# Context rows taken relative to the last one, and short matmul groups given new places in the tile

## What is computed

```python
x = x + xattn(layernorm(x), ctx)    # 16 heads of 16; softmax over 257 context rows
x = x + attn(layernorm(x))          # rms-norm, rotary q and k, sigmoid weights divided by their sum
x = x + moe(layernorm(x))           # gate 256 -> 8, top 1, capacity 160, experts 256 -> 1024 -> 256, gelu

def xattn(query, ctx):
    q, k, v = heads(query @ Wq.T + bq), heads(ctx @ Wk.T + bk), heads(ctx @ Wv.T + bv)
    return merge(softmax(q @ k.T) @ v) @ Wo.T + bo
```

## Time and profile before

| | before |
|---|---|
| median of 3 runs | 1319.5 us (1315.08 to 1319.97) |
| the profiled execution | 1326.8 us, of which its span is 1324.9 us |
| PE matmul / weight load busy | 1160.6 us (88%) / 980.9 us (74%) |
| DVE / ACT / POOL busy | 851.6 us (64%) / 801.9 us (61%) / 568.9 us (43%) |
| mean granted clock of TensorE | 0.946 of full speed |

### The profile page before, as it was taken

How to read it: one execution, slowest core, us unless ns; L and a number is a source line. 1 busy time by engine, 2 the same in 40 slices (tenths; PEclk the granted TensorE clock), 3 DMA queues, 4 the chain that set the end, 5 groups by cost and what they waited for, 6 DMA issues and landing times. The chain is left out here.

```text
span 1324.9 us, 43348 instructions
## 1 busy us (share of the span) xinstructions
PE 1160.6 (88%) x17169; PEld 980.9 (74%) x17169; DVE 851.6 (64%) x2395; ACT 801.9 (61%) x2347; POOL 568.9 (43%) x1045
## 2 busy tenths in 40 slices
PE   6898988989889889999988988998999988874897
PEld 5677777777777777777777777777787777752796
DVE  4667777776776677766677766777666667653111
ACT  5677666666666666666666766766656666632121
POOL 2344444454554444445445444444444544432021
PEclk9999999998999999989999999999888999975899
DMA  6415111111111111111111111111111111000474
GB/s 156 124 46 182 54 58 54 58 57 34 52 50 54 49 36 50 51 47 52 36 47 48 50 51 31 50 50 51 46 45 36 48 50 46 14 10 13 135 227 138
DMA packets 71927, 82.32 MB, mean 62 GB/s; under 512 B 16987, under 2 KB 50732, under 8 KB 71728
## 3 DMA queue, kind: packets, MB, share of 16 engines
q1 hardware_dynamic: 65280, 75.19, 19.3%
q0 software_dynamic: 3200, 3.71, 0.8%
q10 hardware_dynamic: 3248, 0.66, 0.2%
HBM read 64.79 MB, written 16.56 MB: 61 GB/s over the span
## 5 line engine op out<-in xcount | busy, mean ns | idle before, releaser
L735 ACT ACTIVATE prob<-score,nmx 128x257 f32<-128x257 f32 x512 | 236.2, 476 | 219.1 <-DVE nmx L936 218.8
L401 PE MATMUL kps<-ctx_p,wk_p 128*128 128x256 f32 x1536 | 217.4, 292 | 0.3 <-POOL ctx_p L1235 0.2
L411 PE MATMUL vps<-wv_p,ctx_p 128*128 128x256 f32 x1536 | 214.7, 289 | 0.0
L401 PEld LDWEIGHTS kps<-ctx_p,wk_p 128*128 128x128 f32 x1536 | 200.0, 196 | 6.1 <-issue 1.9
L1235 POOL TENSOR_TENSOR ctx_p<-ctxT,ctx_p 128x512 fp32r<-128x512 f32 x128 | 152.3, 1190 | 117.1 <-ACT ctx_p L751 116.7
L411 PEld LDWEIGHTS vps<-wv_p,ctx_p 128*128 128x128 f32 x1536 | 191.5, 191 | 12.4 <-issue 12.4
L936 DVE TENSOR_REDUCE nmx<-score 128x2 f32<-128x514 f32 x256 | 165.2, 687 | 51.7 <-PE score L428 51.7
L1253 POOL TENSOR_TENSOR plast<-const,prob 128x128 f32<-128x128 f32 x128 | 64.1, 501 | 255.8 <-DVE prob L947 255.8
L947 DVE TENSOR_SCALAR prob<-prob,rsum 128x257 f32<-128x257 f32 x512 | 158.5, 352 | 9.0
L953 DVE COPY probT<-score 128x512 f32<-128x512 f32 x96 | 66.4, 691 | 126.2 <-PE score L444 125.9
L444 PE MATMUL score<-const,prob 128*128 128x128 f32 x1024 | 140.8, 281 | 2.3 <-DVE prob L947 2.1
(11 more groups left out here) (159 smaller groups left out, 2029.3 us busy)
## 6 DMA issues: line engine op xcount, KB each, us to landing
ctxT<-in_ctxT SPq DMA_DIRECT2D x128, 257.0 KB, 3.0
w<-in_w SPq DMA_DIRECT2D x16, 1024.0 KB, 8.7
xq<-in_x SPq DMA_DIRECT2D x32, 128.0 KB, 3.2
xr<-in_x SPq DMA_DIRECT2D x32, 128.0 KB, 2.1
qbd<-qkT SPq DMA_DIRECT2D x256, 16.0 KB, 1.9
out<-row SPq DMA_DIRECT2D x32, 128.0 KB, 1.9
slots<-row SPq DMA_DIRECT2D x10, 257.0 KB, 5.6
x_a<-slots SPq DMA_DIRECT2D x8, 129.0 KB, 2.1
```

The lines of the kernel that those rows point to most:

```text
L401: last = mm(kps[:, c, :], wk_p[:, x, n, c * P:(c + 1) * P], ctx_p[:, g, y, n, :], start=(n, x) == (0, LO), stop=(n, y) == (C - 1, LO))
L411: last = mm(vps[:, c, :], ctx_p[:, g, x, n, c * P:(c + 1) * P], wv_p[:, y, n, :], start=(n, x) == (0, LO), stop=(n, y) == (C - 1, LO))
L735: last = af(prob[:, m, :], score[:, m, 0:S], ACT.Exp, bias=nmx[:, m:m + 1], scale=1.0, accum_out=esum[:, m:m + 1])
```

## The change

- **Relative context.** `context_hi` and `context_lo` take `ctx - last row` in place of `ctx`: softmax weights don't change when every score of a row is shifted alike, and they sum to 1, so the last value row is added at the end. Its key column becomes the bias alone, written once. `last_key`, `last_prob`, `last_probs`, `last_values` per tile and `attended` go; the probabilities' last column is no longer normalised.
- **Engines.** `context_hi` on ACT is two instructions of 256 columns with a bias operand where there was one of 512. `context_lo` moves from POOL to DVE as two instructions of 256. The split of `y1T` moves from an ACT copy and two POOL instructions to one on ACT (`rows_hi`) and one on DVE (`rows_lo`), straight from PSUM. The even heads of `extract` move from ACT to DVE. The second half of the rotary products moves from POOL to DVE.
- **PSUM.** `counts` and the transposed rows of the second norm lie in the fourth score bank.
- **Order.** `self_values` runs in three pieces of 6, 5 and 5 heads. Both `project_out` calls run behind `transpose_probs`. `scores2`, `transpose_qk`, `project_queries`, `transpose_queries` and `gate` change places. `choose` (and the exponential of the gate) runs one iteration later, between DVE's `normalise` and its copy of the transposes. On SP, the load of the next `x` comes ahead of the weights, of `xr` and of the second half of the context.

```diff
@@ PE's table between
-                    (0, 0): s1 and (lambda: (turn("att_tmp", t1 + 1), last_probs(t1))),
-                    (0, 1): lambda: (t3 is not None and positions(t3),
-                                     s2 and (turn("relu_done", t2 + 1), scores2(t2))),
-                    (0, 2): s1 and (lambda: (turn("x1_step", 3 * t1 + 1), project_out(att, wo, "att_done", t1, "o1_ps"))),
-                    (0, 3): q and (lambda: (turn("xnT_done", i + 2), transpose_queries(i + 1))),
-                    (1, 0): q and (lambda: (turn("qT_done", i + 2), project_queries(i + 1))),
-                    (1, 1): s1 and (lambda: (spare_free(xa, i, 1), transpose_rows(y1, "y1_done", t1, "y1t_ps", spare_c))),
-                    (1, 2): s2 and (lambda: (turn("att2n_done", t2 + 1), self_values(t2))),
+                    (0, 0): s2 and (lambda: (turn("relu_done", t2 + 1), scores2(t2))),
+                    (0, 2): once(i) and (lambda: (turn("vlast_done", C), last_rows())),
+                    (0, 3): lambda: (s1 and (turn("x1_step", 3 * t1 + 1),
+                                             project_out(att, wo, "ext_step", 2 * t1 + 2, t1, "o1_ps"))),
+                    (1, 0): q and (lambda: (turn("xnT_done", i + 2), transpose_queries(i + 1))),
+                    (1, 1): s2 and (lambda: self_values(t2, range(0, 6))),
+                    (1, 2): lambda: (s2 and self_values(t2, range(6, 11)),
+                                     s1 and (spare_free(xa, i, 1), transpose_rows(y1, "y1_done", t1, "y1t_ps", spare_c)),
+                                     t3 is not None and (spare_free(xa, i, 1, 1), positions(t3))),
+                    (1, 3): s2 and (lambda: self_values(t2, range(11, H))),
-                    (2, 2): s2 and (lambda: (turn("x2_step", 3 * t2 + 1), project_out(att2, ao, "att2_done", t2, "o2_ps"))),
-                    (2, 3): s1 and (lambda: (turn("qkT_done", t1 + 1), transpose_qk(t1))),
-                    (3, 0): s2 and (lambda: (turn("y2T_done", t2 + 1), transpose_rows(row, "y2_done", t2, "y2t_ps", sh_c))),
-                    (3, 1): s2 and (lambda: (turn("logit_done", t2 + 1), gate(t2))),
-                    (3, 3): s1 and (lambda: (spare_free(xa, i, 3), project_v2(t1))),
+                    (2, 3): s2 and (lambda: (turn("x2_step", 3 * t2 + 1),
+                                             project_out(att2, ao, "att2_done", t2 + 1, t2, "o2_ps"))),
+                    (3, 0): s1 and (lambda: (turn("qkT_done", t1 + 1), transpose_qk(t1))),
+                    (3, 1): q and (lambda: (turn("qT_done", i + 2), project_queries(i + 1))),
+                    (3, 2): s2 and (lambda: (spare_free(xa, i, 3, 1), transpose_rows(row, "y2_done", t2, "y2t_ps", spare2_c))),
+                    (3, 3): lambda: (s2 and (turn("logit_done", t2 + 1), gate(t2)),
+                                     s1 and (spare_free(xa, i, 3), project_v2(t1))),
@@ ACT
-                af(ctx_p[:, g, HI, :, :], ctxT[:, r, :, g, 0:SM], ACT.Copy).then_inc(s["ctx_hi"], 1)
+                for c in range(C):
+                    last = af(ctx_p[:, g, HI, c, :], ctxT[:, r, c, g, 0:SM], ACT.Identity, bias=nlast[:, c, b:b + 1], scale=1.0)
+                last.then_inc(s["ctx_hi"], 1)
@@ DVE
+            def context_lo(t, j):
+                b, r, g = TB * t + j, j // 2, j % 2
+                dve.wait_ge(s["ctx_hi"], b + 1)
+                for c in range(C):
+                    last = v.scalar_tensor_tensor(ctx_p[:, g, LO, c, :], ctxT[:, r, c, g, 0:SM], nlast[:, c, b:b + 1],
+                                                  ctx_p[:, g, HI, c, :].bitcast(F32), ALU.add, ALU.subtract)
+                last.then_inc(s["ctx_parts"], 1)
@@ POOL, removed: last_key, context_lo, rows_parts, last_prob, rope_sin
```

More of the change, by code:

```diff
@@ L463, in weighted_values, with project_out @@
                 last.then_inc(s["pv_done"], 1)
[L465 to L475 removed]
+            def project_out(x, w, ready, count, t, done):
+                pe.wait_ge(s[ready], count)
                 for c in range(C):
@@ L529, in self_values @@
                                   start=True, stop=True)
[L530 removed]
+                if heads[-1] == H - 1:
+                    last.then_inc(s["pv2_ps"], 1)
             def gate(t):
@@ L803, in _ @@
             queries(0, 0)
-            act.wait_ge(s["wkv_in"], 16 * 6)
+            act.wait_ge(s["wkv_in"], 16 * 5)
             keys(0, 0)
-            act.wait_ge(s["last_ps"], 1)
-            for c in range(C):
-                last = af(klast[:, c, :], shared[:, c * P:(c + 1) * P], ACT.Identity, bias=b_k[:, c:c + 1], scale=1.0)
-            last.then_inc(s["klast_done"], 1)
             context_hi(0, 1)
@@ new lines, in body @@
+                if xa:
+                    maxima(i, 0)
+                    context_lo(i, 2)
+                if s1:
+                    extract(t1)
+                if once(i):
+                    norm_x(1)
+                if xa:
+                    normalise(i, 0)
+                if i >= 3:
+                    choose(t2 - 1)
+                if xa:
+                    probsT(i, 0)
+                if q:
+                    norm_x_apply(i + 1)
+                if s1:
+                    residual1(t1)
@@ new lines, in body @@
+                if s1:
+                    residual1_stats(t1)
+                    residual1_mean(t1)
+                if once(i):
+                    last_values()
+                if s2:
+                    sigmoid_product(t2)
+                if xa:
+                    maxima(i, 1)
+                if s1:
+                    norm1(t1)
+                if xa:
+                    context_lo(i, 3)
+                if xa:
+                    normalise(i, 1)
+                if xa:
+                    probsT(i, 1)
@@ new lines, in body @@
+                if i >= 3:
+                    position(t2 - 1)
+                if s1:
+                    rows_lo(t1)
+                if s2:
+                    inverse2(t2)
+                    weigh2(t2)
+                if xa:
+                    maxima(i, 2)
+                if s1:
+                    evac_qk(t1)
+                if xa:
+                    normalise(i, 2)
+                if s1:
+                    rope_products(t1)
+                if q:
+                    context_lo(i + 1, 0)
@@ new lines, in body @@
+                if s1:
+                    rope_add(t1)
+                if once(i):
+                    setup_scales()
+                if s2:
+                    residual2(t2)
+                if xa:
+                    maxima(i, 3)
+                if s2:
+                    residual2_stats(t2)
+                    residual2_mean(t2)
+                if q:
+                    context_lo(i + 1, 1)
+                if s2:
+                    norm2(t2)
+                if xa:
+                    normalise(i, 3)
+                    probsT(i, 3)
@@ L1174, in _ @@
+                if norms_ahead(i):
+                    norm_x(i + 2)
+                if s2:
+                    logits(t2)
+                if s1:
+                    evac_v2(t1)
+                if once(i):
+                    setup_parts()
             tiles(body)
+            choose(T - 1)
             position(T - 1)
```

316 lines of the change are left out of this document (104 added, 212 removed).

## The result

| | before | after |
|---|---|---|
| median | 1319.7 us (1315.1 to 1334.9, 4 runs) | 1188.8 us (1186.9 to 1189.8, 4 runs) |
| the profiled execution, its span | 1326.8, 1324.9 us | 1189.8, 1187.6 us |
| PE / DVE / ACT / POOL busy | 88 / 64 / 61 / 43% | 92 / 75 / 68 / 21% |
| mean granted clock of TensorE | 0.946 | 0.966 |

The ratio is 0.902 (95% interval 0.899 to 0.904): 131 us less where 99 were forecast, 1189 for 1220, inside the range and faster as forecast.

A forecast was written before the change was run, and what follows sets the result against it. PE was taken to bound nine tenths of the loop. Tiles fall from 36.53 to 33.4 us (31.2 plus 2.2 of waits), 94 us over 30 tiles, and 5 more: 99 less, 1220 us, range 1180 to 1262.

The forecast's parts named there:

- Part 1: Last-row matmuls leaving PE: 1.0 us per tile, plus waits of 1.13 ahead of scores2 and 0.28 ahead of positions.
- Part 2: Splitting self_values lets the instruction queue fill: 0.94 us of gap and 0.85 of clock loss gone per tile.
- The floor: PE's tile with none of the named losses and no other gap: 31.2 us.
- Part 3: New waits of PE on DVE and ACT across the four sequences: 2.2 us, making 33.4 us per tile.
- Part 4: Queues: diagonal transfers keep about 1 us of cover, sent rows and tile 0 weights arrive in time; free.
- Part 5: Start and end: start nothing, within 3 us; drain 2.5 less, tile 1 gains 2.5; 5 us in all.
- A: DVE becomes the bound, tiles of 34.5 us, 1254 us in total; chance 0.15.
- B: Fetch gaps in PE's small matmuls move on instead of going, 28 us more, 1248 us; chance 0.10.
- C: PE's short groups cover the new waits better, 0.7 for 2.2, tiles of 31.9 us, 1175 us; chance 0.10.
- D: The diagonal lands late for scores2, 1 us late costing 30, 1250 us; chance 0.08.
- E: Each of the three self_values pieces lets the clock fall, 39.6 us a tile, 1407 us, slower; chance 0.04.
- F: Late diagonal, ACT in sequence 3 and evac_qk together give back 3.1 us per tile, about 1320 us; chance 0.03.

The follow-up runs named there:

- One piece: Changed kernel with all 16 heads of self_values in a single stretch again: 1204.2 us, 32.32 us a tile.
- choose-late: Changed kernel with choose behind DVE's copy of the transposes in sequence 0 instead of ahead of it: 1178.1 us.
- y2T-early: Changed kernel with ACT's copy y2T ahead of its copy of the values in sequence 3: 1178.0 us.
- all-three run: Changed kernel with weights first, choose behind DVE's copy and y2T ahead of the values together: 1170.2 us, ratio 0.879 to the kernel before of 1331.9.
- weights first: Changed kernel with SP's weight transfers at tile 0 ahead of its wait for the normalised rows: 1182.8 us.
- low-parts run: Changed kernel with context_lo on POOL again as one subtraction of 512 elements, leaving out the last row: 1182.6 us.
- pieces alone: Kernel before with only self_values split into three pieces: 1337.3 us, ratio 1.044.

## Why the prediction was right, and where it wasn't

- **What bounds the kernel**: right. PE's idle time fell from 3.49 to 0.99 us a tile and the tile from 36.5 to 31.9; taking 3.5 us of work off DVE moved the tile by 0.13.
- **Part 1**: right as far as the rows go: no idle time ahead of `scores2` (0.2 us in 27 tiles) or of `positions`. The 1.0 us for `last_probs` itself was not tested apart from the rest.
- **Part 2, the gap and the clock**: the size was right, the cause wrong, and that the size came right was luck. The step that failed is "the queue of instructions runs dry", read from where the gap stood and how short the matmuls are. POOL's row of the same microsecond was not laid beside it. One piece without the sending beside it has 0.3 us of gap in 27 tiles; the kernel before loses its gap when only the sending moves. In the change this is part 4's edit, `choose` and `position` a place later, which the prediction counted as free. The three pieces themselves are worth 15 to 17 us. Beside the kernel before of 1278.5 us the whole change is worth 92 us: if that kernel ran without the gaps, the 30 x 1.79 = 54 of this part were not there to win.
- **The floor**: 31.91 - 0.99 = 30.9, forecast 31.2, 30 x 0.3 = 9 us.
- **Part 3, the new waits**: the mis-sized term, 2.2 forecast and 0.99 measured, 30 x 1.2 = 36 us. With the 9 of the floor the tiles were forecast 45 us too long; the first tiles took back about 7, and 6 are the difference between the two spans (137) and the two medians (131), which leaves about the 31 by which the forecast was too high. Sequence 0: 0.5 ahead of `weighted_values` and 0.3 in the transposes were forecast, 0.42 and about none came as idle time; the transposes are stretched to 1.32 us, where sequences 1 and 2 have 1.03 to 1.07, but I take it that the wait behind them would be longer without that, so it counts once (no run shows it). Sequence 1: 0.6 forecast, none. Sequence 2: 0.1, none. Sequence 3: 0.7, measured 0.48. I had added the delays of DVE and ACT one by one where each is covered by the same short groups of PE. The choose-late and y2T-early runs show that the two that remain are worth what the rows say.
- **Prices**: `context_lo` 0.88 a pair forecast and 478 ns an operation measured; `pr<-ex,rse`, forecast at 0.23, measures 231 ns; rotary products 0.45, measured 420 ns; DVE 28.0 forecast, 27.1 measured; ACT 24.6, 24.4.
- **Part 4**: the diagonal's cover of about 1 us held, barely, as the all-three run shows. The sent rows were there in time. "Still ahead of DVE's use" for the weights at tile 0 failed: DVE waited 3.7 us, and weights first gives 4 to 6 us back. The sentence compared SP's delay with no row for when DVE comes to its scaling.
- **Part 5**: for the start and the first tiles nothing, within 3, was forecast, and they lost about 7: outside the 27 tiles 11.6 us were won, where three tiles and the 5 of this part make 19. The delay of tile 0 brought tile 1's first scores to 48.34 from 46.02, 2.3 later. Drain 2.5 less, measured 57.0 against 54.9 from the last `weighted_values` to the experts, 2.1.
- **Rivals**: A (DVE bound) falls by the low-parts run. B (gaps move on) falls: no idle time without releaser in the 27 changed tiles; the drain has stops of 3.0 and 1.8 us, where before had one of 3.0. C was right about the length of a tile, 31.9, at the chance of 0.10 I gave it, for the reason it states (0.99 of waits for its 0.7, on a floor 0.3 lower); the first tiles and the span of the traced execution, 7 above the median, kept the total above its 1175. D becomes real at 31.0 us. E falls: the clock over 27 tiles reads 1.00. F falls with the 131 us.

## What to carry to other kernels

An idle time without releaser in a run of small matmuls wants the rows of the other engines' queues in the same microsecond beside it before it is put down to the run itself; moving a GpSimd indirect transfer that is issued there cost one line here, and that alone won 3.4% of the kernel before where it took 1332 us, and nothing where it took 1279. And when one kernel's time differs between groups of runs, trace the reference in each of them. When several engines are late at one place, only the latest counts: take the last wait of each sequence, don't add them. And when a wait is moved ahead of loads on a queue, look up the row in which the first user of those loads runs.

## What the runs showed of the hardware

- POOL's issue of an indirect transfer of 128 rows (1.12 us) beside a run of 32x32 matmuls stopped PE for 0.37 and 0.50 us, in the same place in nearly every tile of both traces of the kernel before; beside the wide matmuls of keys and values it stopped nothing in 27 tiles, and in the run with the pieces alone, taken beside a kernel before of 1278.5 us, its first 0.4 us stopped no small matmul either.
- PE also stops without a releaser and without such an issue beside it: 3.00 and 1.82 us in the drain of the changed kernel, 3.00 with one piece.
- The granted clock fell with those stops: 0.95 over 27 tiles with them, 1.00 without.
- DVE's scaling of 256 fp32 elements by a pointer scalar took 403 to 415 ns in 26 of 27 tiles (832 in the one in which it met a POOL operation) and 1284 on average beside POOL's operation of 512 (`norm2`), and the scalings of the probabilities 365 and 449. The Trainium skill (GPSIMD Engine Reference, section Specifications) has the SBUF interfaces shared between the two, with contention for VectorE's instructions in a 2-port mode or with two inputs in SBUF. The rows agree that they can hold each other up; which of its cases these scalings are no run shows.
- The time of one kernel differed by 4% between groups of runs on different chips (1278.5 and 1331.9 us), and that of its successor, timed in two of them, by 0.2% (1186.7 and 1188.8 us). The part that varied has the size of the stops and of the clock's falls that go with them (1331.9 - 1286.2).
